# Moving steps in a hand-written order: half a product, the next tokens' transposes and the router's stages (attention and mixture of experts, one core)

## What is computed

```
x = x + layernorm(attention(layernorm(x)))     # 16 heads of 128, 4 key/value heads, rope, causal mask
x = x + layernorm(ffn(layernorm(x)))
ffn(t): scores = sigmoid(t @ gate_w); scores_b = scores + bias
        keep 4 of 8 groups by the sum of their 2 best; take the 6 best of the kept experts
        weights = chosen scores / their sum * 2.5
        sum over the chosen experts of weight * (silu(t @ w_gate) * (t @ w_up)) @ w_down, capacity 48 tokens each
        + shared expert: (silu(t @ ws_gate) * (t @ ws_up)) @ ws_down
```

## Time and profile before

| | us |
|---|---|
| median of 3 runs | 2049.85 (2048.86 to 2051.9) |
| the profiled execution, its own time | 2050.17 |
| its span in the profile | 2048.4 |
| PE busy | 1895.5 (93% of the span) |
| DVE busy | 1330.8 (65%) |
| POOL busy | 1284.4 (63%) |
| ACT busy | 1154.0 (56%) |

### The profile page before, as it was taken

How to read it: one execution, slowest core, us unless ns; L and a number is a source line. 1 busy time by engine, 2 the same in 40 slices (tenths; PEclk the granted TensorE clock), 3 DMA queues, 4 the chain that set the end, 5 groups by cost and what they waited for, 6 DMA issues and landing times. The chain is left out here.

```text
span 2048.4 us, 34361 instructions
## 1 busy us (share of the span) xinstructions
PE 1895.5 (93%) x11846; PEld 1566.2 (76%) x11846; DVE 1330.8 (65%) x3149; ACT 1154.0 (56%) x2632; POOL 1284.4 (63%) x1061
## 2 busy tenths in 40 slices
PE   5999999999999999999999999999999999787926
PEld 4888888888888888888888888888888888543412
DVE  5566666667767677777667667676676778762324
ACT  3556666666656665566565665666655655333413
POOL 5758576666666765758485766676666755214733
PEclk8999999999999999999999999999999999995658
DMA  5005000001110100000100100001101000298476
GB/s 178 16 27 164 29 21 6 22 6 31 48 52 6 42 1 22 11 27 32 58 21 6 42 6 27 6 21 57 32 6 42 1 17 17 105 357 284 67 220 210
DMA packets 77292, 120.22 MB, mean 59 GB/s; under 512 B 9639, under 2 KB 57717, under 8 KB 75873
## 3 DMA queue, kind: packets, MB, share of 16 engines
q1 hardware_dynamic: 65264, 92.61, 13.6%
q0 software_dynamic: 7248, 12.72, 2.6%
q10 hardware_dynamic: 4608, 12.68, 1.9%
HBM read 90.34 MB, written 38.53 MB: 63 GB/s over the span
## 5 line engine op out<-in xcount | busy, mean ns | idle before, releaser
L561 PE MATMUL s_ps<-kT,q 128*128 128x512 f32 (+3 forms) x2304 | 584.3, 371 | 13.9 <-POOL q L1136 7.9
L824 DVE TENSOR_TENSOR pT<-t_ps,pT 128x512 fp32r<-128x512 f32 (+3 forms) x768 | 401.0, 550 | 191.0 <-ACT pT L969 189.8
L811 DVE TENSOR_REDUCE neg_max<-s_ps 128x1 f32<-128x640 f32 (+7 forms) x512 | 384.6, 751 | 110.8 <-PE s_ps L561 103.9
L561 PEld LDWEIGHTS s_ps<-kT,q 128*128 128x128 f32 x2304 | 408.3, 192 | 61.6 <-ACT probs L958 11.6
L586 PE MATMUL av_ps<-pT,v 128*128 128x512 f32 x1728 | 442.2, 400 | 2.7 <-DVE pT L824 2.7
L1121 POOL TENSOR_TENSOR k_roped<-raw,sinT 64x512 f32<-64x512 f32 x316 | 406.7, 1287 | 24.3
L969 ACT ACTIVATE pT<-t_ps 128x512 fp32r<-128x512 f32 (+3 forms) x768 | 348.7, 490 | 129.8 <-PE t_ps L571 125.0
L958 ACT ACTIVATE probs<-s_ps,neg_max 128x640 f32<-128x640 f32 (+7 forms) x512 | 381.9, 746 | 63.3 <-DVE neg_max L811 61.0
L586 PEld LDWEIGHTS av_ps<-pT,v 128*128 128x128 f32 x1728 | 311.8, 189 | 67.1 <-DVE pT L824 7.8
L571 PE MATMUL t_ps<-k_ident,probs 128*128 128x128 f32 x2304 | 340.1, 274 | 11.6 <-DVE pT L824 7.9
L1118 POOL TENSOR_TENSOR k_roped<-raw,cosT 128x512 f32<-128x512 f32 x158 | 204.4, 1294 | 220.1 <-ACT raw L930 201.3
(11 more groups left out here) (245 smaller groups left out, 1877.4 us busy)
## 6 DMA issues: line engine op xcount, KB each, us to landing
w_early<-in_expert_w SPq DMA_DIRECT2D x5, 2560.0 KB, 26.6
w_early<-sums SPq DMA_DIRECT2D x24, 512.0 KB, 8.8
k_staged<-in_wpack SPq DMA_DIRECT2D x47, 256.0 KB, 2.9
sums<-sums ACTq DMA_DIRECT2D x2, 4144.0 KB, 22.9
k_staged<-in_wpack SPq DMA_DIRECT2D x16, 512.0 KB, 3.7
e_w_late<-in_expert_w SPq DMA_DIRECT2D x3, 2560.0 KB
k_xw<-in_x SPq DMA_DIRECT2D x4, 1024.0 KB, 5.8
k_xb<-in_x SPq DMA_DIRECT2D x4, 1024.0 KB, 5.9
```

The source lines that it names most:

```text
L561: last = pe.matmul(out, q[:, macro % 2, a, h, int(big)], kT[:, g % 2, s, lo:hi], start=(n == 0), stop=(n == 2))
L811: dve.reduce_max(neg_max[:, r % 16:r % 16 + 1], s_ps[:, r % 2, 0:(row_tile(r) + 1) * P], AX.X, negate=True).then_inc(max_ready, 1)
L824: dve.tensor_tensor(lo, t_ps[n % 2][:, 0:count * P].rearrange("p (j n) -> p j n", n=P), hi.bitcast(F32), ALU.subtract).then_inc(t_lo, 1)
```

## The change

Three tables and two step lists change. The first half of the big tile's product, `av_0`, moves from the end of e5 (after the transposes) to e6, behind the scores of that step and ahead of `next_kv`. `next_x` moves from the end of e6 to e7, behind the scores of that step. The router's stages get other steps, x is scaled at +56 to +62 instead of +39 to +48, and the passes start three steps later.

```
-BEFORE = {0: ('out_0',), 1: ('out_1', 'av_small'), 2: ('q_0',), 3: ('q_1',), 5: ('out_3',), 6: ('next_kv',)}
-AFTER = {3: ('out_2',), 5: ('av_0',), 6: ('av_1', 'next_x')}
+BEFORE = {0: ('out_0',), 1: ('out_1', 'av_small'), 2: ('q_0',), 3: ('q_1',), 5: ('out_3',), 6: ('av_0', 'next_kv'), 7: ('next_x',)}
+AFTER = {3: ('out_2',), 6: ('av_1',)}
 QUAD_STEPS = (   # first quad of a batch, second quad, quad 6
-    dict(..., y_add=(0, 1), ..., x2=(13, 14), logit=(44,), biased=(46,), groups=(48, ..., 53), mask=(55,), top=(56, 57), chosen=(61,), key=(62,), total=(62,), weight=(62,)),
-    dict(..., y_add=(16, 17), ..., x2=(30, 31), logit=(68,), biased=(70,), groups=(73, ..., 78), mask=(78,), top=(87, 88), chosen=(90,), key=(93,), total=(90,), weight=(95,)),
-    dict(y=(-11, -11, -10), y_rstd=(-9,), y_add=(-8, -8), x1=(-7, -7, -6), ..., x2=(-3, -2), logit=(-1,), ..., mask=(3,), ..., key=(6,), total=(6,), weight=(7,)),
+    dict(..., y_add=(1, 2), ..., x2=(14, 15), logit=(46,), biased=(48,), groups=(48, ..., 53), mask=(53,), top=(57, 58), chosen=(60,), key=(62,), total=(65,), weight=(68,)),
+    dict(..., y_add=(16, 17), ..., x2=(30, 31), logit=(63,), biased=(64,), groups=(71, ..., 76), mask=(77,), top=(84, 85), chosen=(89,), key=(94,), total=(94,), weight=(104,)),
+    dict(y=(-11, -11, -10), y_rstd=(-9,), y_add=(-9, -9), x1=(-8, -8, -7), ..., x2=(-2, -1), logit=(-1,), ..., mask=(4,), ..., key=(5,), total=(5,), weight=(5,)),
 )
-X_STEPS = dict(x=(33, 34, 35, 36, 37), x_rstd=(39,), x_apply=(45, 46, 47, 48))
-PASS_STEPS = (97, 100, 103, 106, 109, 112)
+X_STEPS = dict(x=(33, 34, 35, 36, 37), x_rstd=(56,), x_apply=(59, 60, 61, 62))
+PASS_STEPS = (100, 103, 106, 109, 112, 115)
```

More of the change, by code:

```diff
@@ L106 @@
 QUAD_STEPS = (
-    dict(y=(-8, -7, -6), y_rstd=(-3,), y_add=(0, 1), x1=(4, 5, 6), x1_rstd=(9,), x1_apply=(11, 12), x2=(13, 14), logit=(44,), biased=(46,), groups=(48, 49, 50, 51, 52, 53), mask=(55,), top=(56, 57), chosen=(61,), key=(62,), total=(62,), weight=(62,)),
-    dict(y=(12, 13, 14), y_rstd=(14,), y_add=(16, 17), x1=(21, 22, 23), x1_rstd=(24,), x1_apply=(25, 26), x2=(30, 31), logit=(68,), biased=(70,), groups=(73, 74, 75, 76, 77, 78), mask=(78,), top=(87, 88), chosen=(90,), key=(93,), total=(90,), weight=(95,)),
-    dict(y=(-11, -11, -10), y_rstd=(-9,), y_add=(-8, -8), x1=(-7, -7, -6), x1_rstd=(-4,), x1_apply=(-4, -4), x2=(-3, -2), logit=(-1,), biased=(0,), groups=(0, 0, 1, 1, 2, 2), mask=(3,), top=(4, 4), chosen=(5,), key=(6,), total=(6,), weight=(7,)),
+    dict(y=(-8, -7, -6), y_rstd=(-3,), y_add=(1, 2), x1=(4, 5, 6), x1_rstd=(9,), x1_apply=(11, 12), x2=(14, 15), logit=(46,), biased=(48,), groups=(48, 49, 50, 51, 52, 53), mask=(53,), top=(57, 58), chosen=(60,), key=(62,), total=(65,), weight=(68,)),
+    dict(y=(12, 13, 14), y_rstd=(14,), y_add=(16, 17), x1=(21, 22, 23), x1_rstd=(24,), x1_apply=(25, 26), x2=(30, 31), logit=(63,), biased=(64,), groups=(71, 72, 73, 74, 75, 76), mask=(77,), top=(84, 85), chosen=(89,), key=(94,), total=(94,), weight=(104,)),
+    dict(y=(-11, -11, -10), y_rstd=(-9,), y_add=(-9, -9), x1=(-8, -8, -7), x1_rstd=(-4,), x1_apply=(-4, -4), x2=(-2, -1), logit=(-1,), biased=(0,), groups=(0, 0, 1, 1, 2, 2), mask=(4,), top=(4, 4), chosen=(5,), key=(5,), total=(5,), weight=(5,)),
 )
```

## The result

The changed kernel takes 2043.72 us in the median (2041.02 to 2046.04), against 2049.85 for the kernel before: the ratio is 0.9967, with a 95% interval of 0.9957 to 0.9978. It is 6.1 us faster, a little more than the 4.1 us that I had called the bound of what can be told, and faster than the forecast of 2046.5, just inside my own range (2043.5 to 2049.5). The profiled execution took 2041.02 (span 2039.2); it was the quickest of its runs, so its distance to the profile before, 9.1 us, is larger than that of the medians.

The account below looks back on a forecast made before the run. PE, busy 1895.5 of 2048.4 us, was taken as the bound, so only its short waits could change. Gains of 16.7 and losses of 13.4 gave net -3.3: 2046.5 us median, own range 2043.5 to 2049.5, overall 2040 to 2054.

Parts of the forecast that it names:

- rival A: Losses are mostly covered by VectorE's slack; half of 13.4 us comes, 2039.9 us by the median; chance 0.30.
- gain 1: `av_0` behind the last scores, which fill its wait: 0.36 us with m=0, 0.2 with m=1, 7.3 in all.
- gain 2: Logits from +44 and +68 to +46 and +63, without their wait: 0.85 us per batch, 2.5 in all.
- gain 3: Groups' choice from +78 to +76: PE's 1.23 us wait for exponentials goes; 3 x 1.3 = 3.9 us.
- gain 4: At +75 only a small reduction instead of MAX8, 1.2 us; `top` from +87 to +84, 1.8 us.
- loss 1: Residual adds at +2 meet GpSimd's multiplies and delay residues that PE's transposes need: 1.4 x 3 = 4.2 us.
- loss 2: Second quad's first MAX8 at +71 (e7), plus the x residue in batches 1 and 2: 2.1 us.
- loss 4: `next_x`: `out_0` waits for the x residue, now behind a maximum; 0.2 to 0.28 us each, 1.3 in all.
- loss 5: x2 at +14 and +15: its copy queues behind exponentials, PE starts later, half returns at +17; 1.5 us.
- loss 6: Quad 6 and last group: adds waiting for their root 1.0, x2 right before logits 1.0, rope 0.5; 2.5 us.
- B: Moved VectorE work hits PE in full, deciding above 70% of moved time; 2057 us by the median; chance 0.15.
- C: The gain of `av_0` is given back at later GpSimd or ScalarE waits; 2053.9 us by the median; chance 0.10.

Follow-up runs that it names:

- e7: Not a run but a step of a macro: in the kernel before, a pass of 1.7 us there cost PE 1.34 us, leaving slack of 0.38.
- The first experiment: The kernel before with only `av_0` moved behind the scores of the next step, everything else old: 2051.99 us, ratio 1.0005.

## Why the prediction came out as it did

The direction and the mechanism of most terms were right, and the time fell between the forecast and rival A. "Measured" is from the rows, after against before, except where an experiment undid one term:

| term | forecast | measured |
|---|---|---|
| gain 1, `av_0` (its share in gain 2's macros included) | 9.0 | 10.6 |
| the rest of gain 2, logits | 0.8 | 0.7 |
| gain 3, choice of groups | 3.9 | 3.7 |
| gain 4, +75 and `top` | 1.2 + 1.8 | 1.2 + 1.9 |
| loss 1, adds at +2 | 4.2 | 4.05 |
| loss 2, MAX8 at +71 | 2.1 | 1.5 |
| loss 3, passes | 1.8 | 1.7 |
| loss 4, `next_x` | 1.3 | 0.8 |
| loss 5, x2 at +14/+15 | 1.5 | 0.0 |
| loss 6, quad 6 | 2.5 | 4.2, of which 1.6 is clock |
| clock in the first macro | none | gain of 1.5 |

**Gain 1.** Right, and 1.6 too small. I took 0.36 for m=0 and 0.2 for m=1; undoing the move cost 0.42 and 0.24 in the mean, in all 16 macros of each kind (13, and the 3 with logits that gain 2 had counted). Up to `next_kv` it was 0.34 (against the earlier trace rows) to 0.38 (against the kernel with `av_0` put back), as forecast; the rest lies behind that point and was not taken apart. But the prediction treated it as a gain of its own. The first experiment shows it is not: with x2 and key left at e5 their waits took it back in full.

**Gain 2 to gain 4.** As forecast, each within 0.2. At +81 the 1.23 us of the earlier trace rows are gone, at +77 0.41 a batch, at +89 0.52 to 0.67.

**Loss 1.** Right in size (1.35 a batch against 1.4) and in its cause: the add pair took 2.75 us, against "about 2.6" forecast, and moving it one step earlier took the loss away. The Trainium skill's page "SBUF — State Buffer", section "SBUF: two separate sides", which would have VectorE with two SBUF inputs and GpSimd hold the shared ports by turns, agrees with the 2.75 and with the 0.87 of the pairs that meet no multiply.

**Loss 2, 3 and 4.** Right in place; loss 2 came to 0.6, 0.6 and 0.3 instead of 0.93, 0.93 and 0.25. The MAX8s cost 0.3 in every batch, as the slack of 0.38 read from one pass at e7 says; the x residue added 0.28 in batches 1 and 2 (the run with `next_x` back), not its whole 0.68. Otherwise `next_x` costs only at +88. At +79 of batch 1 `out_0` starts 3.18 us after `av_1`'s end (the parts that I had put at 3.25 add up to 3.20), 0.16 later than before, but by the end of +80 nothing of that is left.

**Loss 5** is the term that was wrong. Its first half was right: PE waits 0.73 at +16, and by the end of that step x2's move has cost 0.6 (1.0 at +16 and 0.1 at +15, less 0.5 at +13 and +14), as in my 520.25 against 519.65. But I let 0.5 of it stand, and 0.52 came back at +17 and +18 (0.12 and 0.40; the run with x2 back at +13 gives up the same), where PE in the kernel before had waited 0.25 for residues (at 528.49 in batch 1) and in the changed one does not. Both macros together came out 0.26 to 0.31 shorter, which is gain 1's share there (0.24 to 0.28), so x2 cost nothing. The larger miss is what the term was compared with. I priced x2's move against a kernel in which `av_0` still covered x2 at +13; once `av_0` is gone, leaving x2 there costs 1.6 us a batch at full clock. The move that I had booked as a loss is what makes gain 1 possible.

**Loss 6.** The adds' wait is there as forecast: DVE waited 0.81, PE 2.36. At full clock the stretch from row 504 on lost 2.6 against 2.5 forecast, 1.0 of it x2's (the run with only TensorE's units moved has that alone) and 1.6 the adds', for which I had 1.0 and 0.5 for the ropes; the clock took 1.6 more in this execution. What I called "taken up in part by waits of 0.5 and 1.5" is right: 0.50 stayed and 1.51 shrank to 0.57.

**The clock in the first macro** stood in neither sum. The clock of the kernel before is not full everywhere in attention: from 60 to 70 us its mean is 0.83, and PE's first `av_0` took 4.58 us; in the changed kernel it took 3.02. The window in the kernel before, then in the one after:

```profile
60.00:70.00 10.00, 9.61 (x38) 7.75 (x39) 1.79 (x7) 3.13 (x12) 9.55 (x9) 0.83 0.01 2
```

```profile
60.00:70.00 10.00, 9.45 (x46) 7.84 (x47) 3.06 (x9) 4.22 (x14) 9.55 (x9) 1.00 0.01 2
```

The kernel with `av_0` at its old place and all else new had full clock there as well (3.04 us), so it is not the move of `av_0` that brings it. All eleven experiments have it (2.98 to 3.04 us), the one with `av_0` alone and the one with TensorE's units alone too. So it may be this one execution of the kernel before and no gain of the change at all; that stays open, since there is no second profile of it.

The sum by this table is 19.6 - 12.3 = 7.3 us, against 8.2 by the traces up to the end of attention and 6.1 by the medians. The missing 0.9 was not traced. That is 4.0 better than the forecast's 3.3: 1.6 from gain 1, 1.5 from loss 5 and 1.1 from losses 2 and 4; the two entries of the clock, 1.5 and 1.6, were not forecast and cancel, which is luck. It is not rival A: at full clock 10.7 of the 13.4 us of losses came, not half. B needed over 70% of the moved time to reach PE; loss 1 did, losses 4 and 5 did not. C is excluded by the run with everything but `av_0`. One slip in the chances: A, all of it below the bound, was entered among the faster ones with 0.28 instead of 0.30.

## What to carry to other kernels

Before moving a unit out of a queue, ask what it covers, not only what it waits for: whoever stands behind it and shares a buffer with the unit ahead, or needs a result that is not ready yet, has lived on its duration. A moved step has its price in three places, read each by itself: the queue behind it, the port it shares with another engine at that moment, and the buffer it writes, whose last reader may stand behind something long. And take apart a change that bundles moves: here the moves of TensorE's units alone gave 7.5 us, the router's other moves won and lost about the same, and putting three of them back gave 7.4 us, more than the change itself.

## What the runs showed of the hardware

- VectorE's adds with two SBUF operands and GpSimd's multiplies took turns wherever they met: two adds take 0.87 us alone, 2.75 us beside two multiplies of 1.3; of four in a row three took 0.48 each and the one that met a multiply 1.52, and that multiply itself was stretched from 1.29 to 1.41. Residues of VectorE with one operand in PSUM ran beside the same multiplies in 1.28, as without them.
- After a wait of PE of about 2 us or more the granted clock can fall from the upper of its two levels (2.4 GHz) to the lower (1.2) for a while, and need not: behind waits of 2.36 and 2.35 at the same instruction, one kernel's profile showed a mean of 0.83 over ten us and a product of 3.81 us, another's 1.00 and 2.24; behind the wait of 1.95 at +13, one execution kept full clock in batch 1 and lost it in batches 2 and 3; behind waits of 3.7 us at +70 (groups and passes at other steps) it fell in all three. Such a drop was worth 1.6 us in quad 6, more than most terms of the sum, and a single profile can't be compared to another without looking for it.
